# Gated RWKV mixing and a quantised feed-forward layer on one core: lag weights stored in two layouts, and the second norm divided and ordered otherwise

## The reference, cut to what matters

```python
ek = exp(k);  cur = exp(u + k)                 # k = v = ctx, one decay w and one u per channel
A_t = sum over s != t of e^{(|t-s|-1) w} ek_s v_s   # forward and backward scan together
B_t = sum over s != t of e^{(|t-s|-1) w} ek_s
wkv = (A + cur * v) / (B + cur)
x = x + tanh(g_xattn) * sigmoid(layernorm(x)) * wkv

z = layernorm(x)                               # the second norm
scale = sigmoid(clip_x) * max(abs(z)) / 127    # one maximum over all of z
xq = clip(round(z / scale), -128, 127) * scale
h = fake_quant(silu(xq @ Wg.T) * (xq @ Wu.T))  # again one maximum over all of h
x = x + tanh(g_ffn) * (h @ Wd.T)
```

## Time and profile before

| | us |
|---|---|
| median of 3 runs | 202.14 (200.98 to 203.15) |
| the profiled execution | 202.25 |
| its span in the profile | 200.5 |
| busy: PE, DVE, ACT, POOL | 178.8, 156.9, 141.3, 109.4 |
| moved by DMA | 32.19 MB, at 344 to 358 GB/s in most slices of the first 86 us |

### The profile page before, as it was taken

How to read it: one execution, slowest core, us unless ns; L and a number is a source line. 1 busy time by engine, 2 the same in 40 slices (tenths; PEclk the granted TensorE clock), 3 DMA queues, 4 the chain that set the end, 5 groups by cost and what they waited for, 6 DMA issues and landing times.

```text
span 200.5 us, 3388 instructions
## 1 busy us (share of the span) xinstructions
PE 178.8 (89%) x1198; PEld 130.1 (65%) x1198; DVE 156.9 (78%) x354; ACT 141.3 (70%) x188; POOL 109.4 (55%) x128
## 2 busy tenths in 40 slices
PE   4989997999998999999948978999999996869990
PEld 4844577999997999999525653444343432658770
DVE  0466899176467765999899958599999998999992
ACT  3477796754237675569768989999798971999900
POOL 3330356436335333335689960989867772358893
PEclk9999999999999999999999999999999999999998
DMA  2999999999999999920000000000000000035545
GB/s 70 345 336 354 348 351 346 348 344 305 333 319 344 304 358 350 324 87 0 0 0 3 0 0 2 0 5 0 0 0 0 3 0 0 0 105 174 195 167 201
DMA packets 32896, 32.19 MB, mean 161 GB/s; under 512 B 2288, under 2 KB 32624, under 8 KB 32880
## 3 DMA queue, kind: packets, MB, share of 16 engines
q1 hardware_dynamic: 32464, 31.47, 49.9%
q10 hardware_dynamic: 416, 0.52, 0.7%
HBM read 27.53 MB, written 4.46 MB: 160 GB/s over the span
## 4 chain that ended last, share of the span: by engine, by line
DVE 31%; PE 27%; DMA 14%; POOL 8%; issue 7%; ACT 6%; SPq 4%; POOLq 1%; DVEq 0%; ACTq 0%
PE ps L994 16%; DMA hidden<-lag_w 9%; PE ps L1098 6%; DVE h_peaks L890 6%; DVE z_t L939 6%; DMA hidden<-in_ctx 5%; DVE hidden L879 4%; POOL rs L400 3%; PE ps L981 3%; DVE bn L708 3%; POOL hidden L436 2%; DVE h_space L739 2%; DVE z_t L945 2%; DVE silu_out L945 2%; DVE silu_out L751 1%
## 5 line engine op out<-in xcount | busy, mean ns | idle before, releaser
L994 PE MATMUL ps<-hidden 128*128 128x128 f32 (+1 forms) x512 | 61.2, 282 | 1.9 <-DMA hidden<-lag_w 1.4
L994 PEld LDWEIGHTS ps<-hidden 128*128 128x128 f32 x512 | 60.7, 196 | 2.4 <-DMA hidden<-lag_w 1.6
L410 POOL TENSOR_TENSOR x_all<-x_all,silu_out 128x512 f32<-128x512 f32 x15 | 23.2, 1550 | 36.2 <-DVE silu_out L751 36.2
L739 DVE SCALAR_TENSOR_TENSOR h_space<-z_t,ps 128x256 f32<-128x256 f32 x32 | 18.9, 597 | 16.7 <-PE ps L994 12.6
L890 DVE TENSOR_REDUCE h_peaks<-hidden 128x1 f32<-128x1024 f32 (+1 forms) x24 | 26.0, 1123 | 0.2
L1134 PE MATMUL ps<-wdT,z_t 128*128 128x256 bf16 x192 | 22.4, 273 | 2.8 <-DVE z_t L939 2.5
L515 ACT ACTIVATE up_out<-h_space 128x512 f32<-128x512 f32 x15 | 9.4, 628 | 21.0 <-DVE h_space L739 21.0
L1134 PEld LDWEIGHTS ps<-wdT,z_t 128*128 128x128 bf16 x192 | 17.8, 97 | 7.6 <-DVE z_t L939 3.2
L642 ACT ACTIVATE silu_out<-ps,mix_scale 128x1024 f32<-128x1024 f32 (+1 forms) x18 | 18.3, 1019 | 2.1 <-PE ps L1098 2.0
L507 ACT ACTIVATE z_t<-x_all,mr,nr 128x256 f32<-128x256 f32 x32 | 16.4, 589 | 1.8 <-POOL mr L388 1.8
L662 ACT ACTIVATE h_space<-hidden,small 128x2560 int16<-128x2560 f32 (+1 forms) x9 | 17.1, 1944 | 0.3 <-DVE z_t L939 0.3
(11 more groups left out here) (107 smaller groups left out, 305.6 us busy)
## 6 DMA issues: line engine op xcount, KB each, us to landing
hidden<-lag_w SPq DMA_DIRECT2D x32, 512.0 KB, 7.2
x_all<-in_x SPq DMA_DIRECT2D x8, 512.0 KB, 8.9
hidden<-in_ctx SPq DMA_DIRECT2D x8, 512.0 KB, 9.5
out<-x_all SPq DMA_DIRECT2D x15, 256.0 KB, 2.1
xq<-in_L_ffn_w_down SPq DMA_DIRECT2D x1, 704.0 KB, 6.4
xq<-in_L_ffn_w_gate SPq DMA_DIRECT2D x1, 640.0 KB, 6.0
h_space<-in_L_ffn_w_up SPq DMA_DIRECT2D x1, 640.0 KB, 7.2
out<-x_all ACTq DMA_DIRECT2D x1, 256.0 KB, 2.8
```

The costliest lines, as they stand in the source:

```text
L410: nc.gpsimd.tensor_tensor(xs, xs, mixed[:, m % 2, :, :].rearrange("p c b -> p b c"), ALU.add).then_inc(s["x1_done"], 1)
L739: nc.vector.scalar_tensor_tensor(den[:, m % 2, i * HALF:(i + 1) * HALF].rearrange("p (c b) -> p c b", b=SEQS), ez[:, :, j * CK:(j + 1) * C ...
L994: last = nc.tensor.matmul(ps[:, j % BANKS, c * 2 * SEQS:end * 2 * SEQS], lag_matrix(j, c), ekp[:, (j * CK + c) * 2 * SEQS:(j * CK + end) * ...
```

## The change

1. ScalarE computes the lag weights of the upper 64 partitions once more, in a second tile `alone` in which each channel's 255 values lie by themselves, and stores them in a second DRAM tensor (128 KB). Chunks 18 to 31 are loaded from there. A partition then reads 8 stretches of 128 values (512 bytes) where it read 4 of 1024 bytes; the bytes of a chunk are the same, and `lag_matrix` is contiguous for these chunks.
2. `BY_POOL` becomes 0, 0, 1, 2, 2, ... : groups 0 and 1 are normalised wholly by ScalarE, group 2 keeps one sequence for GpSimd.
3. GpSimd computes the factors of groups 0, 1 and 2-3 in a row, and later batches one step ahead of the groups that it normalises.
4. `tanh_ffn` stands ahead of `normalise(0)`.
5. VectorE takes peaks 1 to 7 behind the last statistics; only peak 0 stays among them.
6. `idle_wide(4)` follows only the first five groups.

```diff
+    ALONE = 18
-    BY_POOL = 1, 1, 1, 2, 2, 2, 2, 2
+    BY_POOL = 0, 0, 1, 2, 2, 2, 2, 2
+    def by_pool(g):
+        return len([i for i in range(g + 1) if BY_POOL[i]])
...
         def lag_matrix(j, c):
-            tile = ring[(GROUPS + j) % SLOTS].rearrange("p (g t i) -> p g i t", t=T, i=SET)
-            return tile[:, c // SET, c % SET, :]
+            tile = ring[(GROUPS + j) % SLOTS]
+            if j >= ALONE:
+                return tile[:, c * T:(c + 1) * T]
+            return tile.rearrange("p (g t i) -> p g i t", t=T, i=SET)[:, c // SET, c % SET, :]
...
+        alone = sb("alone", [P, CG * LAGS])
+        lag_alone = alone[:, :].rearrange("p (i j) -> p i j", i=CG)
+        alone_dram = nc.dram_tensor("lag_alone", [P, CG * LAGS], F32, kind="Internal")
...
-                src = bass.AP(lag_dram, j * CK * LAGS, [[SET, P], [SET * LAGS, CK // SET], [1, SET * T]])
+                set_, dram = (SET, lag_dram) if j < ALONE else (1, alone_dram)
+                if j == ALONE:
+                    sp.wait_ge(s["alone_stored"], 16)
+                src = bass.AP(dram, j * CK * LAGS, [[set_, P], [set_ * LAGS, CK // set_], [1, set_ * T]])
...
             rstd2(0)
-            for i, batch in enumerate(BATCHES):
-                if i == 0:
-                    rstd2(1)
-                for g in batch:
-                    normalise_last(g)
-                if 1 <= i < len(BATCHES) - 1:
-                    rstd2(i + 1)
+            rstd2(1)
+            rstd2(2)
+            normalise_last(2)
+            normalise_last(3)
+            rstd2(3)
+            normalise_last(4)
+            rstd2(4)
+            for g in range(5, GROUPS):
+                normalise_last(g)
...
+            def lag_weights_alone():
+                rows = slice(ALONE * CK // CG // 32 * 32, P)
+                for i in range(CG):
+                    nc.scalar.activation(lag_alone[rows, i, :], lag_row[rows, :], ACT.Exp, scale=wu[rows, i:i + 1]) \
+                        .then_inc(s["alone_done"], 1)
+                act.wait_ge(s["alone_done"], CG)
+                nc.scalar.activation(lag_alone[rows, :, T - 1], wu[rows, CG:2 * CG], ACT.Exp).then_inc(s["alone_done"], 1)
+                act.wait_ge(s["alone_done"], CG + 1)
+                act.dma_start(alone_dram[rows, :], alone[rows, :]).then_inc(s["alone_stored"], 16)
...
             lag_weights()
+            lag_weights_alone()
...
+            tanh_ffn()
             normalise(0)
             normalise(1)
-            tanh_ffn()
...
             for g in range(GROUPS):
                 if g == 4:
                     peak_z(0)
-                if g >= 6:
-                    peak_z(g - 5)
                 late_stats(g)
                 if g == 0:
                     early_stats(SEQS - 2, 2)
-            for g in range(GROUPS - 5, GROUPS):
+            for g in range(1, GROUPS):
                 peak_z(g)
...
-                if g < GROUPS - 1:
+                if g < 5:
                     idle_wide(4)
```

More of the change, by code:

```diff
@@ L241, in gated_rwkv_ffn @@
             "gate_in", "up_in", "down_in", "g_x_in", "g_f_in", "clx_in", "cld_in", "w_in", "u_in",
-            "ones_set", "ident_set", "flip_set", "lags_set", "lag_done", "lag_stored",
+            "ones_set", "ident_set", "flip_set", "lags_set", "lag_done", "lag_stored", "alone_done", "alone_stored",
             "tanh_done", "clips_done", "prep",
@@ L299, in load_lags @@
                     sp.wait_ge(s["ab_done"], before - GROUPS + 1)
-                src = bass.AP(lag_dram, j * CK * LAGS, [[SET, P], [SET * LAGS, CK // SET], [1, SET * T]])
-                sp.dma_start(ring[(GROUPS + j) % SLOTS].rearrange("p (g n) -> p g n", n=SET * T), src).then_inc(ring_in[(GROUPS + j) % SLOTS], 16)
+                set_, dram = (SET, lag_dram) if j < ALONE else (1, alone_dram)
+                if j == ALONE:
+                    sp.wait_ge(s["alone_stored"], 16)
+                src = bass.AP(dram, j * CK * LAGS, [[set_, P], [set_ * LAGS, CK // set_], [1, set_ * T]])
+                sp.dma_start(ring[(GROUPS + j) % SLOTS].rearrange("p (g n) -> p g n", n=set_ * T), src).then_inc(ring_in[(GROUPS + j) % SLOTS], 16)
             def load_weights(m):
@@ L764, in peak_z @@
                 dve.wait_ge(s["z_done"], g + 1)
-                dve.wait_ge(s["z_last"], g + 1)
+                wait(dve, s["z_last"], by_pool(g))
                 nc.vector.tensor_reduce(peaks[:, g:g + 1], z_all[:, g * GC:(g + 1) * GC], AX.X, ALU.max,
@@ L1010, in turn_z @@
                 pe.wait_ge(s["z_done"], g + 1)
-                pe.wait_ge(s["z_last"], g + 1)
+                wait(pe, s["z_last"], by_pool(g))
                 if g == 1:
```

## The result

The changed kernel takes 203.81 us in the median, where before took 202.06 in the same runs: an estimated ratio of 1.0079, 95% interval 1.0054 to 1.0103, so about 1.6 us slower (the quotient of the two medians is 1.0087, inside the interval). The prediction had 200.5, a range up to 202.4, and 0.69 on "within 1%". The profiled execution took 203.83 us, its span is 202.1 (before 200.5).

The account below looks back on a forecast made before the run. VectorE was taken to bound mixing behind chunk 23, and a chain through GpSimd the second norm. Lag part -0.38 and norm part -1.28 sum to -1.66 us, a median of 200.5 us, range 199.7 to 202.4.

Parts of the forecast that it names:

- The norm part: Second norm: reordered GpSimd, ScalarE and VectorE work ends the last peak 1.28 us sooner, bounds 0.7 to 1.6.
- x = 0.18, so chunk 23 lands at 77.08: Lag loads: each short-packet chunk takes 0.18 us longer; six move chunk 23's landing from 76.0 to 77.08 us.
- The line through the neighbours: Lag loads: a line through 18 ns (256 bytes) and 45 ns (1024 bytes) gives 27 ns per 512-byte packet.
- the engines had room: Lag loads: with the engines' own limit about 385 GB/s, 348 leaves room, so a chunk could take 1.60 us, x = 0.09.
- SP's wait for the store is long satisfied; what is queued behind it are chunks: SP's queue at chunk 18: the wait for the second table's store costs nothing; chunks and the third weight follow.
- rival of expensive packets: Lag loads: 512-byte packets cost clearly more than 27 ns, chunk 23 lands late, TensorE and VectorE wait; chance 0.10.
- idle time of TensorE for loads between chunks 18 and 31: Mixing stage: a sign named beforehand that would show the prediction wrong; no size given.
- 0.10 for the second table and its store: Early load stream: the added 128 KB store costs 0.1 us, taken between 0 and 0.37.
- part 1: Mixing stage, separate matrices for chunks 18 to 31: -0.48 + 0.10 = -0.38 us, between -0.59 and +0.4.
- The stride: TensorE, chunks 18 to 31: contiguous reads take 111.5 ns a record instead of 117.8, 0.10 us less a chunk.
- The rival on the other side: Lag loads: long packets were the cheaper ones, so the kernel gets slower, about 210 us at 40 ns a packet; chance 0.10.
- part 2: Second norm: the new order of work on GpSimd, ScalarE and VectorE, forecast at -1.28 us.

Follow-up runs that it names:

- the kernel with 1.66: Changed kernel, chunks 18 to 31 in short packets but read by TensorE with a stride of two values (wrong matrices); 1.0042 of the kernel before.
- the norm part alone: Second norm as changed, all lag chunks from the interleaved table without a second table, against the kernel before: 0.9925, 199.95 against 201.30 us.
- the lag part alone: Only the second table and short packets for chunks 18 to 31, second norm as before, against the kernel before: 1.0125, 203.76 against 201.30 us.

## Why the prediction was wrong, by its own steps

**The norm part was right**: 1.40 us in the profile where 1.28 were forecast, and each of its reasons held when tried: the table load is free in ScalarE's gap and worth 0.5 us together with the rest but nothing alone, and the peaks behind the statistics are worth 0.45. The other 0.45 is left to GpSimd's new order and shares by subtraction; no run takes these apart, nor the idle products that were dropped.

**The step that failed is the landing of chunk 23 under short packets, in the sum "x = 0.18, so chunk 23 lands at 77.08", with the wait and the clock that hang on it.** It landed at 79.16. It was missed in three ways, of which only the first is a size:

1. The packets. The line through the neighbours gave 27 ns, which was then eased to 1.69 us a chunk on the argument that at 348 GB/s the engines had room. Measured are 291 GB/s, 1.80 us a chunk, x = 0.29, just outside the upper end of 0.27. The room was not there. Six chunks make 1.8 us; TensorE had 1.45 us of slack at chunk 23 (77.46 - 76.0), and the faster records took 0.49 of it away.
2. The queue ahead of the stream. The prediction counted transfers as a stream that is always fed ("SP's wait for the store is long satisfied; what is queued behind it are chunks"). With twice the descriptors for a chunk SP's queue took new work more slowly, 3.30 us for the issue of chunk 20 where it was 0.36 (that room for descriptors is what lacked is inferred; that it needs the short packets is shown, since the same move of the values brings nothing with long ones), the single values stood in it, and the engines ran dry: 111 GB/s for 2 us, where 291 are the level, is 1.2 us of stream. Taking the values off the queue gave 1.2 us back by the medians, together with what the clock had cost.
3. The clock. The prediction looked at it only where it drops the idle products (1.00 there), and its rival of expensive packets only let TensorE wait. With 2.4 us of waiting it lost half its clock for 3.4 us, and chunk 23 took 3.2 us, not 1.8.

By the prediction's own sum the size alone would not have done it: at x = 0.29 it has chunk 23 landing at 77.74 and done 0.2 us later than before, and the total at -1.28 + 0.10 + 0.18 = -1.0, so 201.1, inside its range. The hole and the clock, which it had at nothing, are worth another 1.2 us by the medians. And with both gone the kernel was still measured at 202.5, 1.4 more than this sum, of which the table shows 0.4; the rest stays open.

The sum by the profile: TensorE starts chunk 23 at 79.20 and not at 77.46, +1.74; from there to the denominator 3.50 where 2.08 were, +1.42; together 3.16. Less 1.40 of the norm, 1.76, and the span grew by 1.6. The prediction named "idle time of TensorE for loads between chunks 18 and 31" as a sign of being wrong, and that sign came, 2.42 us of it. Its 0.10 for the second table and its store fits what the kernel with short packets from chunk 24 shows.

**The reading of the bound was right and cut both ways.** VectorE is busy behind chunk 23 in every kernel, so all the slack of later chunks was worth nothing, and the delay of this one chunk came through whole. The prediction said that part 1 counts only by when chunk 23 is done; it took the point for the place of a gain and priced the loss there by one number.

**The stride** was right, 111.6 ns a record, and so was what it brings where chunk 23 does not wait for its load (0.58 us, forecast 0.59). The Trainium skill, "TensorE: Matmul & The Clock Gate", "LDWEIGHTS (loading the stationary operand)", counts only the columns of a weight load and so has both layouts alike; the spacing of these float32 records is 111.6 against 117.8 ns, and the measurement decides. The Trainium skill, "DMA: Bandwidth & Descriptors", "Specifications", gives 512 bytes as the least transfer for line rate; here packets of 512 bytes reach 291 GB/s where those of 1024 reach 348.

**The rival on the other side** was the right one, in its mechanism. Its turning point was put at x = 0.47, where part 2 is eaten up; the kernel got there at x = 0.29, because the hole and the clock were not in it. It had a chance of 0.10, and half of that above 203. The sum for 40 ns a packet (about 210 us) was not needed: a packet took 28 ns.

The best kernel that keeps the computation is the norm part alone: 0.9925 of before, or 0.9915 with the values on ScalarE's queue, which is the same.

## What to carry to other kernels

Where a transfer's packets get shorter, count three things: what a packet costs in a saturated stream, how many descriptors the issuing queue then holds, with what stands in it, and whether the engine that waits keeps its clock. Find the one item at which the bound changes over (here the last chunk before VectorE takes over) and spell out the loss there as carefully as the gain; here a slack of 1.45 us was no cover for six loads that were 0.29 us longer each, while the eight behind them cost nothing. Speeding up the engine that waits for a late load only makes it wait longer. And look at single executions: where a clock falls in some and not in others, the median hides two groups, and one profile shows one of them.

## What the runs showed of the hardware that was not expected

- Packets of 512 bytes in a saturated load stream: 291 GB/s, against 348 for 1024 bytes, 64 packets for an engine in 1.80 us, 28 ns each; their own times in the trace are longer (1151 in 116.9% of 32 us, 32 ns each), since they overlap.
- An issue on SP's queue took longer with twice the descriptors: 1.00, 2.42 and 3.30 us for chunks 18 to 20, where they took 0.36 each before. For chunks 26 to 31 it is 1.7 to 2.0 us each, about the 1.80 that a chunk's transfer takes.
- Ahead of chunk 23 the granted clock fell to 0.5 for 3.4 us in the three profiles in which TensorE had stood still for 2.31 to 2.53 us. The fall began 0.3 us before the chunk's first record, 0.1 us behind it, and 1.46 us behind it. It did not come in the profiles with 1.66 and 0.99 us of idle time (one each), but by the mean clocks it came in some executions of the kernel with 1.66.
- Ahead of the first transposes of the second norm TensorE stands still for 2.43 to 2.75 us in all fourteen profiles. The clock fell 0.2 to 1.1 us behind the start of these transposes in four of them and stayed at 1.00 in ten, those of before and after included. So the length of the pause alone does not decide. In the second norm the fall costs nothing: the lag part alone has it, as this window shows (columns as above), and its last peak ends 20.52 us behind GpSimd's first factors, before 20.51.

```profile
107.00:110.30 3.30, 3.30 (x13) 2.33 (x12) 3.23 (x18) 2.81 (x5) 2.97 (x6) 0.50 0.00 0
```

- A float32 stationary operand read with a stride of two values: 117.8 ns a record; contiguous: 111.6.
